# A four-layer graph kernel whose last two layers become two programs with the adjacency resident

## The reference, cut to what matters

```python
h = relu(layernorm(x)); x = x + L1(h, adj, ...)       # ends in (Y - mu) / sqrt(var + eps) * gamma + beta
h = relu(layernorm(x)); x = x + L2(h, adj, W, b)
h = relu(layernorm(x)); x = x + L3(h, adj, weight)

def L2(x, adj, W, b):                   # deg = row sums of adj, dis = (deg + 1e-8) ** -0.5
    return ((dis[:, None] * adj * dis[None, :]) @ x) @ W.T + b
def L3(x, adj, weight):                 # d = row sums of (adj + I) to the power -0.5
    return relu(((adj + I) * d[:, None] * d[None, :]) @ (x @ weight))
```

## Time and profile before

| what | value |
|---|---|
| median of three runs | 3735.41 us |
| the profiled execution | 3734.03 us |
| its span (first to last instruction) | 3732.2 us |
| PE busy | 2939.7 us, 79% |
| DVE busy | 2372.3 us, 64% |
| ACT busy | 1250.2 us, 33% |
| granted PE clock, mean | 0.919 of 2.4 GHz |

### The profile page before, as it was taken

How to read it: one execution, slowest core, us unless ns; L and a number is a source line. 1 busy time by engine, 2 the same in 40 slices (tenths; PEclk the granted TensorE clock), 3 DMA queues, 4 the chain that set the end, 5 groups by cost and what they waited for, 6 DMA issues and landing times. The chain is left out here.

```text
span 3732.2 us, 58601 instructions
## 1 busy us (share of the span) xinstructions
PE 2939.7 (79%) x20312; PEld 2136.5 (57%) x20312; DVE 2372.3 (64%) x4629; ACT 1250.2 (33%) x1684; POOL 63.4 (2%) x76
## 2 busy tenths in 40 slices
PE   1449999999999999999995668857775776851868
PEld 1236676767667676766763346645453655641757
DVE  7975555565555555555554798896879877856130
ACT  3433434434334344434442223323143343311020
POOL 0000000000000000000000000000000000003000
PEclk9969999999999999999997789978887888976989
DMA  5755848476584848658484111010110101000415
GB/s 189 294 220 134 199 99 201 112 186 160 138 200 102 196 107 195 152 146 200 95 201 104 40 46 38 31 35 1 35 42 1 35 12 46 24 4 28 147 61 179
DMA packets 587058, 413.70 MB, mean 111 GB/s; under 512 B 538291, under 2 KB 550838, under 8 KB 559030
## 3 DMA queue, kind: packets, MB, share of 16 engines
q1 hardware_dynamic: 584918, 397.51, 39.7%
q10 hardware_dynamic: 2016, 14.68, 1.0%
HBM read 240.10 MB, written 37.81 MB: 74 GB/s over the span
## 5 line engine op out<-in xcount | busy, mean ns | idle before, releaser
L672 DVE SCALAR_TENSOR_TENSOR e_lo<-e,e_hi 128x2048 f16<-128x2048 f32 x128 | 293.3, 2291 | 456.8 <-ACT e_hi L600 456.8
L554 PE MATMUL av<-vw_hi,pT_hi 128*128 128x256 f16 x2048 | 559.9, 273 | 7.5 <-DMA pT_lo<-e_lo 7.5
L554 PE MATMUL av<-vw_lo,pT_hi 128*128 128x256 f16 x2048 | 559.9, 273 | 0.0
L554 PE MATMUL av<-vw_hi,pT_lo 128*128 128x256 f16 x2048 | 559.9, 273 | 0.0
L543 PE MATMUL logits<-kT_hi,qT_hi 128*128 128x512 f16 x1024 | 389.7, 381 | 7.2 <-DVE att_small L658 5.5
L1565 DVE SCALAR_TENSOR_TENSOR nuc_junk<-nuc_e,nuc_thr 128x2048 bf16<-128x2048 f32 x168 | 388.4, 2348 | 5.8 <-issue 1.3
L543 PE MATMUL logits<-kT_lo,qT_hi 128*128 128x512 f16 x1024 | 388.7, 380 | 0.0
L543 PE MATMUL logits<-kT_hi,qT_lo 128*128 128x512 f16 x1024 | 388.7, 380 | 0.0
L594 ACT ACTIVATE att_small<-att_small,minus 128x1 f32<-128x1 f32 x128 | 37.7, 294 | 828.6 <-DVE att_small L667 828.6
L595 ACT ACTIVATE e<-e,att_small,sc 128x2048 f32<-128x2048 f32 x128 | 266.1, 2079 | 0.0
L600 ACT ACTIVATE e_hi<-e 128x2048 f16<-128x2048 f32 x128 | 244.6, 1911 | 15.3
(11 more groups left out here) (410 smaller groups left out, 5985.7 us busy)
## 6 DMA issues: line engine op xcount, KB each, us to landing
bias<-bias_scratch SPq DMA_DIRECT2D x130, 1028.0 KB, 4.8
bias_scratch<-adj_bias SPq DMA_DIRECT2D x16, 1028.0 KB, 3.9
adjT_scratch<-adjT SPq DMA_DIRECT2D x16, 1024.0 KB, 6.9
nuc_at_hi<-adjT_scratch SPq DMA_DIRECT2D x32, 512.0 KB, 3.9
nuc_at_lo<-adjT_scratch SPq DMA_DIRECT2D x32, 512.0 KB, 4.8
l2d_at<-adjT_scratch SPq DMA_DIRECT2D x16, 1024.0 KB, 4.8
l3d_at<-adjT_scratch SPq DMA_DIRECT2D x16, 1024.0 KB, 4.9
adj_rows<-in_adj_dram ACTq DMA_DIRECT2D x14, 1024.0 KB, 8.6
```

The lines of the kernel that those rows point to most:

```text
L554: last = nc.tensor.matmul(AV[par][:, :], PT[par][w][:, m, :], VW[x][:, m, :], start=(m == 0 and w == x == 0), stop=(m == T - 1 and w == 1))
L672: nc.vector.scalar_tensor_tensor(out=EL[:, :], in0=E[par][:, :], scalar=P_SCALE, in1=EH[:, :], op0=ALU.mult, op1=ALU.subtract).then_inc(lo ...
```

## The change

Seven phases (l1out, last_weights, l2h, l2d, l3h, l3d, finish) become two.

`onward` works by quads of four tiles: the last norm of layer 1, the norm of layer 2, transposes, the product with the layer 2 output weight, and the cut into parts. So the output weight is applied ahead of the diffusion. SP issues the loads of the whole adjacency (16 DMAs of 1 MB) into one resident buffer `AT`; nothing in `onward` waits for them.

`last` does both diffusions out of `AT`. Its PE stream places the transposes and weight products of layer 3 for a quad between tiles of layer 2. The first 12 of 16 source tiles of the first four layer 3 tiles are multiplied before the last quad of features is there. Each tile of the result is stored when it is done.

`prepare` now adds beta ahead of its store (`shifted`), on DVE, and stores in four pieces. The POOL additions of beta go from the end of layer 1.

```diff
-            phase(normalize_onto, "l1out", Y, halfp, gb, acc, x_d)
-            phase(last_weights, a, ident, wT, bb, scales, l2_in, l3_in, l3_out)
-            phase(refresh, "l2h", acc, H, ident, halfp, norm=True, parts=Hq, rows=l2_in[:, :], bias=(acc, bb), lo_gain=LO_GAIN)
-            phase(diffuse, "l2d", at_d, ident, None, acc, Hq, DEG_SCALE, scales[:, 2, :], wT, LO_GAIN)
-            phase(refresh, "l3h", acc, H, ident, halfp, norm=True, weight=a["L3_gnn_weight"], parts=Hq, rows=l3_in[:, :])
-            phase(diffuse, "l3d", at_d, ident, ident16, acc, Hq, 1.0, l3_out[:, :], None, None)
-        phase(finish, acc, out)
+            AT = sb(c, "adjT", [P, T, 2, T, P], F16)
+            phase(onward, a, Y, acc, x_d, at_d, AT, at_here, ident, halfp, gb, scales, W3, bb, l2_out, l3_in, l3_out, Hq)
+            phase(last, AT, at_here, ident, ident16, halfp, W3, bb, acc, Y, Hq, l2_out, l3_in, l3_out, out)
...
 (prepare, SP)
-                sp.dma_start(x_d, acc[:, :, :]).then_inc(stored, 16)
+                for b in range(4):
+                    sp.wait_ge(beta_in, 4 * b + 4)
+                    sp.dma_start(x_d[:, 4 * b:4 * b + 4, :], shifted[:, 4 * b:4 * b + 4, :]).then_inc(stored, 16)
 (prepare, DVE)
+                for t in range(T):
+                    nc.vector.tensor_tensor(shifted[:, t, :], acc[:, t, :], gb[:, 1, :], ALU.add).then_inc(beta_in, 1)
...
+ (onward, SP, behind its loads of weights and features)
+                for t in range(T):
+                    sp.dma_start(AT[:, t, :, :, :].rearrange("p x m n -> p (x m n)"), at_d[t, :, :]).then_inc(at_here[t], 16)
+ (onward, ACT)
+                def cut(b):
+                    s.wait_ge(prod_s, b + 1)
+                    if b == 0:
+                        s.wait_ge(rows_done, 1)
+                    for t in range(QUAD * b, QUAD * (b + 1)):
+                        nc.scalar.activation(Hq[0][:, t, :], product_of(t), ACT.Copy, scale=l2_in[:, 0, t:t + 1]).then_inc(cut_s, 1)
+                        if b:
+                            s.wait_ge(lo_s, t - QUAD + 1)
+                        nc.scalar.activation(rest[:, t % QUAD, :], product_of(t), ACT.Copy, scale=l2_in[:, 1, t:t + 1]).then_inc(cut_s, 1)
+                normal(0)
+                copy(0)
+                for b in range(1, QUADS):
+                    normal(b)
+                    cut(b - 1)
+                    copy(b)
+                cut(QUADS - 1)
+ (onward, DVE, its order)
+                stats_of(0, 0); stats_of(0, 1); centre(0); onto(0); stats_of(1, 0); weights_in()
+                stats_of(0, 2); centre(1); aim(0); onto(1); stats_of(1, 1); weights_out()
+                stats_of(0, 3); centre(2); aim(1); onto(2); stats_of(1, 2); centre(3); aim(2)
+                remainder(0); onto(3); stats_of(1, 3); remainder(1); aim(3); remainder(2); remainder(3)
...
+ (last, PE)
+                def third(t, tiles):
+                    if tiles[0] == 0:
+                        if t < 4:
+                            pe.wait_ge(added, EARLY + t + 1)
+                        else:
+                            pe.wait_ge(xs_s, t - 3)
+                    pe.wait_ge(lo_s, tiles[-1] + 1)
+                    for m in tiles:
+                        for x, y in ((0, 0), (1, 0), (0, 1)):
+                            nc.tensor.matmul(PR[t % 4][:, 0:D], AT[:, t, x, m, :], Gq[y][:, m, :], start=(m == x == y == 0), stop=False)
...
+                for t in range(T):
+                    second(t)
+                    if t >= QUAD + 1 and t % QUAD == 1:
+                        turn(t // QUAD - 1)
+                    if t >= QUAD + 2 and t % QUAD == 2:
+                        weigh(t // QUAD - 1)
+                early, late = range(0, EARLY), range(EARLY, T)
+                third(0, early); third(1, early); turn(QUADS - 1); third(2, early)
+                weigh(QUADS - 1); third(3, early)
+                for t in range(4):
+                    third(t, late)
+                for t in range(4, T):
+                    third(t, range(T))
+ (last, SP)
+                for t in range(T):
+                    sp.wait_ge(final, t + 1)
+                    sp.dma_start(nodes(out)[:, t // 2, t % 2, :], acc[:, t, :]).then_inc(stored, 16)
```

More of the change, by code:

```diff
@@ L54 @@
 FIRST_AT, CLIP = 0.3, 0.1
+L2_ROOM = 128.0
 BELOW_LOW = 0.02
@@ L828, in _, with turn @@
             @block.tensor
             def _(pe):
-                pe.wait_ge(loaded, 48)
+                def turn(b):
+                    pe.wait_ge(made, QUAD * (b + 1))
+                    if b >= 2:
+                        pe.wait_ge(xt_s, KC * (b - 1))
+                    for k in range(KC):
+                        for m in range(QUAD):
+                            last = nc.tensor.transpose(TP[b % 2][k][:, m * P:(m + 1) * P], H[:, QUAD * b + m, k * P:(k + 1) * P], ident[:, :])
+                    last.then_inc(tp_s, 1)
@@ new lines, in products @@
+                def products(b):
+                    pe.wait_ge(xt_s, KC * (b + 1))
+                    if b:
+                        pe.wait_ge(cut_s, 2 * QUAD * b)
+                    for m in range(QUAD):
+                        for k in range(KC):
+                            last = nc.tensor.matmul(product_of(m), xT[b % 2][:, k, m * P:(m + 1) * P], wT[:, k, :],
+                                                    start=(k == 0), stop=(k == 1))
+                    last.then_inc(prod_s, 1)
@@ L831, in _ @@
+                pe.wait_ge(w_loaded, 48)
                 pe.wait_ge(one, 1)
@@ L833, in _ @@
                     for o in range(KC):
[L834 to L840, removed]
+                        nc.tensor.transpose(w_tp[:, k * D + o * P:k * D + (o + 1) * P], w2[:, o, k * P:(k + 1) * P], ident[:, :])
@@ new lines, in aim, with remainder @@
+                def aim(b):
+                    q = slice(QUAD * b, QUAD * (b + 1))
+                    v.wait_ge(powed, ASKS.index((1, b)) + 1)
+                    nc.vector.scalar_tensor_tensor(out=minus[:, q], in0=mv[:, 1, q, 0], scalar=-1.0, in1=rstd[:, 1, q],
+                                                   op0=ALU.mult, op1=ALU.mult).then_inc(aimed, 1)
+                def remainder(b):
+                    for t in range(QUAD * b, QUAD * (b + 1)):
+                        v.wait_ge(cut_s, 2 * t + 2)
+                        nc.vector.scalar_tensor_tensor(out=Hq[1][:, t, :], in0=Hq[0][:, t, :], scalar=-LO_GAIN, in1=rest[:, t % QUAD, :],
+                                                       op0=ALU.mult, op1=ALU.add).then_inc(lo_s, 1)
@@ new lines, in _ @@
+                nc.vector.memset(ones[:, :], 1.0).then_inc(one, 1)
+                stats_of(0, 0)
+                stats_of(0, 1)
+                centre(0)
+                onto(0)
+                stats_of(1, 0)
+                weights_in()
+                stats_of(0, 2)
+                centre(1)
+                aim(0)
+                onto(1)
+                stats_of(1, 1)
+                weights_out()
+                stats_of(0, 3)
+                centre(2)
+                aim(1)
```

426 lines of the change are left out of this document (254 added, 172 removed).

## The result

Four runs of the changed kernel have a median of 3667.53 us (3665.78 to 3668.13), four of the kernel before on the same chip 3734.95 (3733.48 to 3735.55). The ratio is 0.9818 [0.9804, 0.9832]: 67.4 us less. The forecast was 3660 in a range of 3649 to 3676. The profiled execution took 3668.13, its span 3666.1.

A forecast was written before the change was run, and what follows sets the result against it. The last 352.6 us were taken as six stretches limited by DVE, PE or waits. Onward to 3453.1, 1.3 between, 195.0 of diffusions and the end gave 3653.1, with prepare's 3.9 a span of 3657.0; median 3660, range 3649 to 3676.

The forecast's parts named there:

- The diffusions: In last, first to last matmul: layer 2 tiles 83.8, layer 3 tiles 90.2, layer 3's rows 18.9, cold start 2.1; 195.0 us.
- The join: In last, between layer 2 and layer 3: a chain of 5.3 us, at most 7.3, covered by 8.1 us of matmuls.
- rival (c): In last, the join isn't covered and matmul groups wait for the last quad: 5 to 8 us more, 3667; chance 0.05.
- the adjacency: 16 MB loaded during onward, 40 to 78 us by rate, each tile landing before its diffusion needs it; costed at nothing.
- Onward: New first stage of the tail: 73.5 us to 3453.1 against 75.1 before, then 1.3 us to the first matmul of last.
- the ring starts when DVE has aimed quad 1: In onward, PE and ACT's quad rounds start after 25 us of DVE work, with one us of waiting for powers.
- rival (a): Onward slower from half clock through every product and powers near 2.92 held back by DVE: 12 us more, 3672; chance 0.14.
- The ring's PE order: In onward, products of quad b-1 stand behind transposes of quad b on PE; a round of 12.5 us, three rounds 37.5.
- Prepare: Beta's 16 additions and the last 512 KB store lengthen prepare: 3.9 us lost, between 2 and 8.
- layer 1 starting about 4 us later: Sign named as showing the forecast right, alongside the 3.9 us forecast as lost in prepare.
- The end: Behind the last matmul: ACT 0.48, DVE 0.42, a 128 KB store at 2.6 and 0.2 of handovers; 9.3 us before.
- rival (d): In last, adjacency tiles arrive late; at 10.5 us each the last lands 26 us late, 3686; chance 0.01.

The follow-up runs named there:

- e4: Changed kernel with the last quad's transposes and weight products straight behind the last layer 2 tile, no layer 3 matmuls covering them; 3678.22 us, one execution.
- e2: Changed kernel with the weights' maxima found in prepare and reduced by its all-reduce, leaving POOL only powers in onward; median 3653.52 us, ratio 0.9779.
- e6: New PE order and weights' maxima in prepare together, plus a spare POOL power in the phase before onward, against the changed kernel; median 3634.36 us, ratio 0.9731.
- e3: Changed kernel with the 16 adjacency loads held back in onward until POOL's sixth power is done; 3660.83 us, one execution.
- e1: Changed kernel with each quad's products behind its own transposes on PE in onward, instead of the next quad's transposes first; median 3650.9 us, ratio 0.9771.
- second set of runs: The changed kernel run once more, unaltered, on the chip of the later follow-up runs as their yardstick; median 3667.2 us, ratio 0.982.

## Why the prediction was right, and where it was not

**The diffusions.** Forecast 195.0 us, measured 191.1, with no hole. By the chain, the layer 2 part with its cold start is 86.4 (forecast 85.9), the rows of layer 3 are 4 x (0.87 + 3.46) = 17.3 (18.9), and 16 tiles of layer 3 are 16 x 5.46 = 87.4 (90.2). The last difference is a reading error: 5.41 in the earlier trace rows is a group with the end of its last matmul, while the next group starts 5.24 after its start, as the earlier trace rows had it (the same chain of the kernel before has a group of 5.25 at 3699.30, with no wait in front). Durations of such groups must not be added up.

**The join and the adjacency.** The chain at the join took 5.3 as forecast, but with other parts: ACT's four passes 2.08 instead of 1.3, DVE's part and the handovers less. What the join would cost without its cover was priced too low, "about 5" and 5 to 8 in rival (c): e4 shows 12, because the waits for the copy and the cut (1.17 and 2.71) then lie bare as well, and the clock falls. The 16 MB came at 407 GB/s on average and were there at about 3437.3, 34 us before the first tile's matmul. PE waited for none of it.

**Onward: the term that was mis-sized.** Forecast 74.8 us from DVE's first instruction to the first matmul (3379.6 to 3454.4), measured 86.7. The step that failed is "the ring starts when DVE has aimed quad 1", with "one us of waiting for the first powers: 25". The aim came after 37.6 us (3384.37 to 3421.96): DVE waited 3.23, 2.76 and 7.28 us for POOL, 13.3 instead of one; the rest, DVE's own work, was 24.3 against 24. (Against the forecast the miss is 11.6, because it counts its 25 us from 3380.6, where DVE's first row stands at 3379.64; no row carries that 1.0 us.) From there to the first matmul it was 49.1 against 48.8: rounds of 12.6 and 13.1 against 12.5, powers of four columns 1.01 against 0.9. The first round came out with other parts than forecast: ACT's normal 2.1 for 1.3, the products 4.8 for 4.6, the transposes 1.8 for 2.1 and the cut 2.9 for 3.3. e2 took the two later waits away, 10.0 of the 13.3 us, and e6 2.2 of the first. The trace of before had shown the price twice: the power of l1out began after "issue", 3.0 us after it was asked for, and so did the all-reduce of `prepare`, for which DVE waited 5.95 us. POOL's timeline of the kernel before:

```profile
2025.62 0.41 POOL L799 PARTITION_ALL_REDUCE deg_ratio_top<-deg_ratio_top  x1 [5.93 <-issue]
```

I had read both as idle time without a price, and counted for POOL only instructions. The lost 12 us have the place and the price of rival (a) but not its cause, so that its number came out is luck: POOL was held up by its own changes of function, lengthened by the loads (e3), not by the clock, whose part in the ring had been forecast. To its own end the stage takes 85.8 us, past the 85 that the prediction had named as wrong.

**A cost that was forecast and not questioned.** The ring's PE order was in the forecast (12.5 per round), and the prediction did not ask whether it need be; e1 shows 13.6 us there. It did not make up for the miss.

**Prepare.** Forecast 3.9. From the attention's last DVE instruction to the first statistics behind `prepare` it was 22.66 us before (2005.52 to 2028.18), and now 24.79. DVE's timeline of the changed kernel, to be set beside the earlier trace rows:

```profile
2007.45 0.48 DVE L678 SCALAR_TENSOR_TENSOR acc<-av,att_small,acc 128x256 f32<-128x256 f32 x1 [11.86 <-PE av L549]
...
2023.15 5.46 DVE L784 TENSOR_TENSOR y<-acc,gamma_beta 128x256 f32<-128x256 f32 x16
...
2032.24 2.06 DVE L99 BATCH_NORM_STATS2 qk_stats<-acc 128x6 f32<-128x256 f32 x6 [2.59 <-PEq L126]
```

That is 2.1 lost. The 16 additions lie in the time in which DVE had waited for the all-reduce, and the last piece's store with the start of the phase takes 3.6 (from 2028.6), not 5. The tail begins 4.7 later than before; the remaining 2.6 came in stages that the change doesn't touch, 1.9 of it ahead of `prepare`. In the second set of runs the same kernel's tail began at 3381.53, so this is how executions differ. It also means that the sign "layer 1 starting about 4 us later" (4.06 here) came true by luck.

**The end.** Forecast 3.7 behind the last matmul, measured 4.0.

**The sum.** In terms of the span: the tail's start 0.9 later than forecast, onward 11.9 more, diffusions 3.9 less, end 0.3 more: 9.2, and the span was 3666.1 against 3657.0. The time fell within the range of 3649 to 3676 because the range kept 12 us for a slower onward, with another cause in mind; without the 3.9 us of the diffusions it would have been about 3671, still within. That it also fell within the forecast's own 3653 to 3668 is luck: it rests on errors of opposite sign, and 2.8 of the 3.9 us that the diffusions gave back are a misread row.

**Slips in the working.** 6 x 1.9 is 11.4 and not 11.6; 2026.8 + 4.2 is 2031.0 and not 2031.2; the round lists 0.5 of handovers and takes 0.2; 3.47 for 16 transposes is 0.22 each, 1.7 times the 0.13 and not twice; and rival (d), at 3686, would still have been 48 us faster than before. None moves the time by more than 1 us.

## What to carry to other kernels

A change of function on POOL (here from powers to an all-reduce and back) is a step with a price of its own, 6 to 11 us in these traces, which in the timeline only the idle time before the next instruction shows, as "issue"; keep one function within a stage that others wait for, gather the reductions where nothing waits for them, or trigger the change in an earlier stage. In a ring of quads over PE and ACT, a quad's products behind its own transposes leave ACT's normal out of the round; in e1 the last two groups of transposes, no longer behind 6 us of idle time, also ran at full clock (1.04 us for 1.97). Work that a later layer needs costs only PE's own time where other matmuls cover its whole latency, and the number of matmuls needed for this can be taken from the chain (5.3 us here, under 7.9).

## What the runs showed of the hardware

- POOL's idle time at a change of function was 7.60 us to a power and 6.12 to an all-reduce with the DMA engines quiet (e3), and 10.45 and 10.95 with them at a share of 1.02 and 417 to 420 GB/s. At a share of 0.79 and 263 GB/s the first change of the changed kernel's `onward` took 7.65.
- A power over four columns takes 1.01 us where one over 16 takes 2.92. Beside a DVE pass that reads two SBUF operands it takes 1.17 (3425.72, beside the centre pass from 3425.55 to 3427.22), so the pass cost it 0.16 us. The prediction had drawn on the Trainium skill (SBUF — State Buffer, "Who interferes with whom"), by which the loser of the shared port blocks wholly, and on the earlier trace rows; it took four passes as one block, up to 1.6 us. No row of `onward` shows such a block; a wait for the rest of one pass of 0.42 us would fit the 0.16, but that isn't shown. Why the power of 16 columns in l1out took 6.18 stays open; it wasn't tried.
- One core loaded 16 MB from DRAM into SBUF at 407 GB/s on average (3396.3 to 3437.3 in the changed kernel) and at 417 to 420 in its middle, while a 1 MB tile of layer 3 before, with at most a few loads in flight, took 4.9 us (median) from issue to landing.
